# Value projections of fourteen head pairs moved to seven-block products with DMA transposes, in a float32-accurate decoder layer on one Trainium2 core

## The reference, cut to what matters

```python
qkv = silu(x @ qkv_w.T).reshape(b, s, 32, 3, 128)     # q, k, v of 32 heads
scores = (q @ k.T) * decay[h]                         # causal, decays with distance
attn   = scores @ v                                   # no softmax
attn   = norm_w * rms_norm(attn over all heads)
gate   = sigmoid(x @ gate_w.T)
x = layernorm(x + (gate * attn) @ out_w.T)
x = layernorm(x + fake_quant(x) @ fake_quant(ctx_4096))
x = layernorm(x + ffn(x[:, perm])[:, unperm])         # 16 small gelu blocks
```

## Time and profile before

| What | Value |
|---|---|
| median of 3 runs | 2036.39 us (2036.36 to 2037.01) |
| the profiled execution: its time | 2038.2 us |
| the profiled execution: its span | 2036.3 us |
| TensorE matmul busy | 1912.5 us, 94% |
| VectorE busy | 1256.3 us, 62% |
| ScalarE busy | 849.1 us, 42% |
| GpSimd busy | 443.3 us, 22% |
| share of the chain that ended last | TensorE 85%, VectorE 6%, ScalarE 4% |
| mean granted TensorE clock | 0.984 |

### The profile page before, as it was taken

The page is one execution under the profiler, slowest core; times in us unless marked ns, Lnnn a source line. Parts: engine busy times, 40 slices in busy tenths (PEclk is TensorE's granted clock), DMA queues, the critical chain, the costliest instruction groups (busy, mean ns, idle before and its releaser), DMA issues.

```text
span 2036.3 us, 28062 instructions
## 1 busy us (share of the span) xinstructions
PE 1912.5 (94%) x10842; PEld 1039.7 (51%) x10849; DVE 1256.3 (62%) x1769; ACT 849.1 (42%) x1255; POOL 443.3 (22%) x356
## 2 busy tenths in 40 slices
PE   6789999999999999999999999999999999986895
PEld 4344646464555646464645555464646465543421
DVE  7566575757575766757565657566565656568533
ACT  4443444435352434444343525343444435314552
POOL 4222121212012121212110201212121111012354
PEclk9999999999999999999999999999999999998898
DMA  4112131222112120212211111202121121401311
GB/s 167 44 37 96 42 104 42 73 68 78 52 63 83 42 89 36 104 42 73 73 42 52 63 52 42 73 22 73 42 73 42 42 73 42 174 33 52 104 57 67
DMA packets 44386, 134.01 MB, mean 66 GB/s; under 512 B 3424, under 2 KB 11744, under 8 KB 41440
## 3 DMA queue, kind: packets, MB, share of 16 engines
q1 hardware_dynamic: 32800, 119.55, 17.1%
q0 software_dynamic: 2560, 8.39, 1.3%
q10 hardware_dynamic: 8896, 4.28, 0.7%
HBM read 119.63 MB, written 12.58 MB: 65 GB/s over the span
## 4 chain that ended last, share of the span: by engine, by line
PE 85%; DVE 6%; ACT 4%; issue 3%; POOL 1%; DMA 0%; ACTq 0%; DVEq 0%; POOLq 0%
PE bank L999 19%; PE bank L1022 13%; PE bank L1023 13%; PE bank L1024 13%; PE bank L1039 5%; PE bank L1041 5%; PE bank L1040 5%; PE bank L1066 2%; PE bank L1064 1%; PE bank L1065 1%; PE bank L1133 1%; PE bank L1141 1%; DVE bank L1375 1%; DVE bank L1390 1%; ACT gate_units L1195 1%
## 5 line engine op out<-in xcount | busy, mean ns | idle before, releaser
L1022 PE MATMUL bank<-x_blocks,w_pair 128*128 128x512 f16 x1344 | 512.1, 381 | 29.2 <-DVE bank L1319 11.3
L1023 PE MATMUL bank<-x_blocks,w_pair 128*128 128x512 f16 x1344 | 512.2, 381 | 0.0
L1024 PE MATMUL bank<-x_blocks,w_pair 128*128 128x512 f16 x1344 | 511.7, 381 | 0.0
L999 PE MATMUL bank<-w_vo,gated_split 128*128 128x512 f16 x1440 | 323.4, 379 | 19.0 <-issue 13.8
L1039 PE MATMUL bank<-w_vo,x_blocks 128*128 128x256 f16 x1024 | 280.4, 274 | 11.3 <-DVE w_vo L1286 8.8
L1040 PE MATMUL bank<-w_vo,x_blocks 128*128 128x256 f16 x1024 | 280.4, 274 | 0.0
L1041 PE MATMUL bank<-w_vo,x_blocks 128*128 128x256 f16 x1024 | 280.4, 274 | 0.0
L1484 POOL TENSOR_TENSOR sums_pair<-raw_pair 128x512 f32<-128x512 f32 x48 | 68.7, 1432 | 902.1 <-DVE w_pair L1286 557.5
L999 PEld LDWEIGHTS bank<-w_vo,gated_split 128*128 128x128 f16 x1440 | 139.6, 98 | 187.8 <-issue 15.8
L1022 PEld LDWEIGHTS bank<-x_blocks,w_pair 128*128 128x128 f16 x1344 | 132.1, 98 | 187.4 <-ACT gate_units L1195 15.4
L1024 PEld LDWEIGHTS bank<-x_blocks,w_pair 128*128 128x128 f16 x1344 | 132.0, 98 | 160.3 <-issue 2.9
(11 more groups left out here) (167 smaller groups left out, 2523.0 us busy)
## 6 DMA issues: line engine op xcount, KB each, us to landing
raw_pair<-w_qk SPq DMA_DIRECT2D x32, 1024.0 KB, 5.1
raw_pair<-w_v SPq DMA_DIRECT2D x16, 1024.0 KB, 4.9
raw_pair<-w_gate SPq DMA_DIRECT2D x16, 1024.0 KB, 4.9
raw_pair<-w_out SPq DMA_DIRECT2D x16, 1024.0 KB, 4.9
decay_sb<-decay SPq DMA_DIRECT2D x32, 256.0 KB, 5.3
raw_pair<-ctx_in SPq DMA_DIRECT2D x8, 1024.0 KB, 4.9
acc<-x_t SPq DMA_DIRECT2D x4, 1024.0 KB, 11.1
ctx<-raw_pair SPq DMA_DIRECT2D x8, 512.0 KB, 2.7
```

Source lines behind the costliest of these rows:

```text
L999: last = pe.matmul(out, a, b, start=m == 1, stop=m == n)
L1022: pe.matmul(bank[:, :], w_hi, x_hi, start=fresh and k == 0, stop=False, skip_group_check=not fresh)
L1023: pe.matmul(bank[:, :], w_hi, x_lo, start=False, stop=False, skip_group_check=not fresh)
L1024: mm = pe.matmul(bank[:, :], w_lo, x_hi, start=False, stop=k == QT - 1, skip_group_check=not fresh)
```

## The change

Values of pairs 1 to 14 get a product phase of their own, like gate, q and k, behind the k phase. Pairs 0 and 15 keep the old form. The weights of the two heads are stored in reverse order, so that results 2 and 3 belong to the pair's first head and results 0 and 1 to its second. Each result goes through the silu to a unit of 128 x 1024 float16 (high part, low part) with the features on the partitions, and one DMA transpose from SP turns it into `v_split` in token order. The four units lie in tiles that are idle then: unit 0 in `scores_split`, units 1 to 3 in `w_vo`. So the scores' high part waits for the turn of unit 0, and the split of the output weights for the turns of units 1 to 3. `attend` waits for the two turns of its head in place of the old silu. The 16 output sums stand in the q phase (0 to 5), the k phase (6 to 11) and the new v phase (12 to 15). Both halves of the context step move to p1 of the k phase.

```diff
+    def v_out(self, r):
+
+        done, place, sign = self.result(r)
+        lo = self.silu(done, place, sign, ("v_unit", r), self.s_free if r == 0 else self.vo_free)
+        self.release(place, lo)
+        self.add("v_turn", r=r, ready=lo, free=max(self.v_hl_free))
+        self.v_turned[r] = self.tick(f"v_turned{r}", 16)
+        if r == 0:
+            self.s_free = self.v_turned[r]
+        if r == 1:
+            self.v_done = [[self.v_turned[2:], self.v_turned[:2]] for _ in range(B)]
...
-                 free=self.t_mm[6] if late else self.vo_free, hi=self.tick("w_hi"))
+                 free=[self.t_mm[6]] if late else [self.vo_free] + self.v_turned[1:], hi=self.tick("w_hi"))
...
         items += [("gate", n), ("q", n), ("o", n - 1)]
+        items += [("k", n)]
         if n <= B * KT // 2:
             items += [("ctx", (n - 1) // QT, (n - 1) % QT)]
-        items += [("k", n), ("v", n)]
+        items += [("vt", n)]
...
-            "p3": [gate(1), split_vo] + ([plan.stash_scale] if stash else []),
+            "p3": [gate(1), split_vo],
         })
...
-            "p1": [attend(3)] + out(0, 1) + gate_rest + ([stash_round] if stash else []),
+            "p1": [attend(3)] + out(0, 1) + gate_rest,
             "p7": [part(0)],
             "p6": out(2, 3) + [part(1)],
             "p5": out(4, 5),
-            "p4": [part(2)] + out(6, 7),
-            "p3": out(8, 9, 10, 11, 12, 13, 14, 15),
+            "p4": [part(2)],
         })
...
         product_pair("k", n, ...
-            "p1": [split_vo],
+            "p1": out(6, 7) + ([stash] if stashing else []),
             "p2": [part(0)],
-            "p6": [value(0)],
-            "p5": [part(1)],
-            "p3": [part(2), value(1)],
+            "p6": out(8, 9),
+            "p5": [part(1)] + out(10, 11),
+            "p3": [part(2)],
         })
+        if not (first or last):
+            product_pair("v", n, {
+                "p1": out(12, 13),
+                "p2": [part(0)],
+                "p6": out(14, 15),
+                "p5": [part(1)],
+                "p3": [part(2)],
+            })
...
+        elif kind == "v_turn":
+            r = st["r"]
+            sp.wait_ge(sem["qkv_lo"], st["ready"][1])
+            until(sp, sem, st["free"])
+            sp.dma_start(c.v_hl[:, r % 2, :, :, :, 1 - r // 2].rearrange("p n b i d -> p (n b i) d"),
+                         c.v_units[r], transpose=True).then_inc(sem[f"v_turned{r}"], 16)
...
         elif kind == "attend":
-            pe.wait_ge(sem["qkv_lo"], st["v"][1])
+            for token in st["v"]:
+                until(pe, sem, token)
```

More of the change, by code:

```diff
@@ L297, in end_v @@
         bank = v["banks"][half]
-        self.v_done[v["b"]] = self.silu(v["mm"][half], bank, 1.0, ("v", v["b"], half), self.v_hl_free[v["b"]])
-        self.main_ring.give(bank, self.v_done[v["b"]])
+        done = self.silu(v["mm"][half], bank, 1.0, ("v", v["b"], half), self.v_hl_free[v["b"]])
+        self.v_done[v["b"]] = [[done]] * GH
+        self.main_ring.give(bank, done)
     def values(self, b):
@@ L328, in attend @@
         self.sig_at += 1
-        st = self.add("attend", h=h, b=b, bank=bank, free=free, s=self.s_ready, v=self.v_done[b], gi=gi,
+        st = self.add("attend", h=h, b=b, bank=bank, free=free, s=self.s_ready, v=self.v_done[b][h % GH], gi=gi,
                       mm=self.tick("attend_mm"), sq_free=self.sig_free[gi], sq=self.tick("sq"),
@@ L572, in split_pair @@
     def split_pair(part):
-        if plan.unsplit and plan.unsplit[0]["what"][0] in ("gate", "q", "k"):
+        if plan.unsplit and plan.unsplit[0]["what"][0] in ("gate", "q", "k", "vt"):
             plan.split_pair(part)
@@ L581, in split_vo, with stash @@
         load_next()
-    def stash_round():
+    def stash():
+        plan.stash_scale()
         plan.stash_round()
@@ L637, in out @@
         def out(r):
-            if kind != "gate":
+            if kind == "v":
+                plan.v_out(r)
+            elif kind != "gate":
                 plan.qk_out(kind, r)
@@ L669, in main_part @@
     for n in range(NG):
-        first, last, stash = n == 0, n == NG - 1, 0 < n <= B * KT // 2
+        first, last, stashing = n == 0, n == NG - 1, 0 < n <= B * KT // 2
         def score(i):
@@ L840, in __init__ @@
         self.s_hl = sb("scores_split", [P, 2, N_SCORES], F16)
-        self.v_hl = [sb(f"v_split{b}", [P, 2, ST, GH * HD], F16) for b in range(B)]
+        self.v_hl = sb("v_split", [P, 2, 2, B, 2, GH, HD], F16)
         self.g_hl = [sb(f"gated_split{b}", [P, GH, 2, S], F16) for b in range(B)]
@@ L878, in __init__ @@
         self.sums = ([t[:, :] for t in self.sig32], [self.gates[:, 0, i] for i in range(2)])
-        self.hid = [self.v_hl[b][:, :, :, :].rearrange("p a s n -> p (a s n)")[:, i * 2 * S:(i + 1) * 2 * S].bitcast(F32)
-                    for b in range(B) for i in range(2)]
+        v_flat = self.v_hl[:, :, :, :, :, :, :].rearrange("p h n b i g d -> p (h n b i g d)")
+        self.hid = [v_flat[:, i * 2 * S:(i + 1) * 2 * S].bitcast(F32) for i in range(4)]
+        vo_flat = self.vo[:, :, :].rearrange("p n m -> p (n m)")
+        self.v_units = [self.s_hl[:, :, :].rearrange("p n s -> p (n s)")[:, 0:2 * S]]
+        self.v_units += [vo_flat[:, i * 2 * S:(i + 1) * 2 * S] for i in range(3)]
         self.hid += [self.g_hl[b][:, i].rearrange("p n s -> p (n s)").bitcast(F32) for b in range(B) for i in range(GH)]
@@ L931, in split_target @@
         if dst[0] == "v":
-            return [self.v_hl[dst[1]][:, n, 2 * dst[2]:2 * dst[2] + 2].rearrange("p s m -> p (s m)") for n in range(2)]
+            return [self.v_hl[:, dst[2], n, dst[1]].rearrange("p i g d -> p (i g d)") for n in range(2)]
+        if dst[0] == "v_unit":
+            return [self.v_units[dst[1]][:, n * S:(n + 1) * S] for n in range(2)]
         name, r = dst
@@ L1173, in scalar_program @@
             src, (hi, _) = c.vo_part(st["part"], st["slot"], st["late"])
-            until(act, sem, st["free"])
+            for token in st["free"]:
+                until(act, sem, token)
             act.wait_ge(sem[st["ready"][0]], st["ready"][1])
@@ L1194, in scalar_program @@
             until(act, sem, st["free"])
-            act.activation(c.gates[:, r // 2, :, r % 2 * HT:(r % 2 + 1) * HT], batches(c.placed(st["place"])), ACT.Sigmoid,
+            dst = c.gates[:, r // 2, :, r % 2 * HT:(r % 2 + 1) * HT]
+            act.activation(dst, like(c.placed(st["place"]), dst), ACT.Sigmoid,
                            scale=st["sign"] / W_SCALE).then_inc(sem["gate_sig"])
@@ L1207, in scalar_program @@
             until(act, sem, st["free"])
-            act.activation(dst, src if len(dst.shape) == 2 else batches(src), ACT.Copy).then_inc(sem["qkv_hi"])
+            act.activation(dst, like(src, dst), ACT.Copy).then_inc(sem["qkv_hi"])
         elif kind == "scores":
```

22 lines of the change are left out of this document (12 added, 10 removed).

## The result

The changed kernel took 2051.36 us (median of 4, 2048.81 to 2052.64) against 2036.7 for the kernel before on the same chip: a ratio of 1.0067, 95% interval 1.0055 to 1.0079. It is slower by about 14 us where 6 us of gain were forecast. The profiled execution has a span of 2049.7 us, 13.4 more than before.

What follows compares the result with a forecast made beforehand. TensorE was taken as the bound; savings less uncovered stalls gave 7.2 us less in pairs 1 to 8 and 1.4 more in pairs 9 to 14, together 5.8 less: 2036.4 becomes 2030.6, said as 2031, range 2008 to 2062.

Steps and rivals of the forecast that it cites:

- The 1.33 us of `stash_scale`: Q phase, pairs 1 to 8: product 7 waits for a gate result behind this ACT step; moving it saves 1.33 us.
- The first uncovered place: V to gate phase: product 7 waits 2.23 us for its weights' split, then `attend(0)` 0.63 more; 2.86 us a pair.
- The second: K to v phase: product 7 waits for part 2 of its weights, 0.2 us a pair.
- The fourth: The DMA transposes of the values: each under 5.6 us, hidden before `attend(0)`, priced at nothing.
- the likeliest case: The gains and stalls come out as worked out: 2024 to 2036 us, chance 0.45.
- the sum: Pairs 1 to 8 save 0.90 us each, pairs 9 to 14 lose 0.23 each: 5.8 us less together.
- rival (b): Granted clock falls behind the new gate-phase stall: 2036 us with falls in five pairs, 2048 in all 14; chance 0.18.
- The third place: Product 5 after product 6, pairs 1 to 8: `u3` late from context steps beside POOL's sums, 0.2 us.
- the upper end: Top of the range for product 5's wait on `u3`: the row's full 2.02 us less 0.2 of slack.

Runs made afterwards that it cites:

- v_early: Changed kernel with the v phase's three splits of the next gate weights moved from p2, p5, p3 to p7, p2, p6: 2001.26 us.
- kv_early: v_early with the k phase's splits also moved early, the context step in p3 of the k phase and value weights loaded before the context block: 1990.13 us.
- before_stash: Kernel before the change with only `stash_scale` moved, from the end of the gate phase to p1 of the q phase: 2025.77 us.
- sums_q: Changed kernel with all 16 output sums left in the q phase, as before the change: 2192.99 us.
- kv_early_vo: kv_early with the first half of the split of the output weights moved from p3 to p5 of the gate phase: 1989.09 us.
- stash_late: Changed kernel with the context step moved from p1 to p3 of the k phase and the context block loaded after the value weights: 2041.21 us.
- filler3: Changed kernel with three matmuls whose result nobody reads added behind product 1 of the gate phase in pairs 2 to 15: 2038.02 us.

## Why the prediction was wrong

**Right.** TensorE as the bound and the pair as the unit: the products save 2.83 us a pair, and v_early and kv_early show it to within 0.3 (pairs of 107.92 and 107.53 us). The 1.33 us of `stash_scale`: before_stash gave 11.3 us against 10.6. The first uncovered place, 2.23 forecast and 2.25 measured, with 0.63 and 0.59 for `attend(0)`. The second, 0.2 forecast and 0.29 measured. The fourth, that turns are hidden: they landed in 3.1 us (median; 4.4 at most) and cost nothing even doubled. The estimate of 1 us of transfer, from the rate in the Trainium skill (DMA: Bandwidth & Descriptors, Latency and other measured facts), is below the 3.1 us; no run here separates the transfer from the rest. The Trainium skill also rates transposes of the hardware queue as the worse ones (Advanced Engine Details and Errata, DGE: Hardware vs Software); against a plain copy on the same queue they took 3.1 us and not 2.9, and no run here has a transpose of the software kind to compare. A pair without context and without a fall lasts 110.55 us, where 110.5 was forecast. The 2051 us lie inside the wide range, 2008 to 2062, but outside the 2024 to 2036 of the likeliest case, and on the other side of the kernel before.

**Wrong: the clock.** The step that failed is the choice between the sum and rival (b): the sum had no term for a fall of the granted clock behind the new stall, and 11 of 14 pairs had one. "The new stall of 2.23 us is nearly as long" as the stretch of 2.40 us after which the clock had fallen was the evidence. I set against it the stall of 2.03 us without a fall, and took "Falls in five pairs" as the middle of a rival with chance 0.18. The 11 falls cost 1.11 us each, 12.2 us: the price of one was nearly right (1.2), the count was not. The trace of before has a nearer stall that the working did not use: TensorE starts again at 1824.80 after 2.29 us, and the clock falls within the next 4 us.

```profile
1824.80:1828.80 4.00, 3.55 (x12) 1.51 (x13) 2.06 (x4) 0.00 (x0) 0.57 (x1) 0.72 0.00 0
```

With that row the fall belonged into the sum with a price. How many of the 14 stalls bring one could not be read from it, and 11 is a count of this kernel: in sums_q it was 26 of 56. The sign that was named for it, "the clock is below 1.00 in mid-run", came.

**Wrong: a size.** The third place was priced at 0.2 us in pairs 1 to 8 and measured 0.87, 5.4 us more in all. The mechanism (the context step beside POOL's sums) was right. What I took too small was the chain: the slowed sums end late and meet the next split, which pays again. That split takes 1.03 us longer (2.25 against 1.22), and less the 0.2 of slack this is the 0.87. The row of 2.02 us in the earlier trace rows was read wrongly too: it is a whole duration, of which 1.22 is there without POOL, so it stood for 0.6 us of stall and not for the 1.8 of the upper end.

The two together are 12.2 + 5.4 = 17.6 us. The second place, 0.09 us a pair more than forecast, makes 1.3, so 18.9 in all. The forecast put the profiled span at 2036.3 - 5.8 = 2030.5 and it was 2049.7, 19.2 more. The sign was lost to two terms that were both named. The five forecast falls of rival (b) give 2037 and not 2036, which changes nothing.

## What to carry to other kernels

A long block of matmuls may be doing two jobs, its own and hiding the work of other engines; when it is replaced by something shorter, list what runs on ACT and VectorE behind it and when each result is wanted. Here a stall of 2.25 us had a second price in the granted clock in 11 of 14 pairs, which slices of the page are too coarse to show; look at stretches of 4 us behind the stall. Moving three weight splits of the v phase a few products earlier turned a loss of 14 us into a gain of 36 (v_early). With those of the k phase and the context step moved as well it was 47 us (kv_early, 1990 us, the fastest kernel together with kv_early_vo), 11 of which the context step also gave in the kernel before.

## What the runs showed of the hardware

- A DMA transpose of a 128 x 1024 float16 unit within SBUF landed 3.1 us after its issue (median of 56 in the changed kernel, 4.4 at most; up to 7.1 in stash_late), a plain copy of the same bytes 2.9; the issue itself takes 1.23 us on SP, against 0.38 for a plain load.
- The granted clock fell after 2.25 us of idleness in 11 of 14 pairs, and never after 1.61 (14 times in filler3) or 2.03. A longer wait did not always bring it down: in sums_q it fell behind 26 of 56 waits of 2.26 to 3.9 us, and behind waits of 2.44 us both happened in one execution. What decides between them no run here shows.
- A low clock hides other waits: with it the wait of `attend(0)`, 0.59 us, vanished, so a fall cost 1.11 us and not the 1.7 that it took from the matmuls.
- POOL's sums and VectorE's work between SBUF tiles slow each other: 2.06 to 2.25 us a sum in place of 1.27, 2.17 us a rounding step in place of 1.23, 2.25 us a split in place of 1.22. It is not always both: the fourth sum kept its 1.26 beside the split that took 2.25. Neither is slower beside VectorE work that reads PSUM (sums 1.26 to 1.28 us, VectorE 0.69 either way).
